# Tokenizer of a four-layer tower: loads ahead of the constants, two inputs prepared first, another order of joins, turns and projections

## The reference

```python
h = layernorm(x.reshape(b, t, j * 3), ln0_g, ln0_b).reshape(b, t, j, 3)
h = jax.nn.relu(conv2d(h, conv1_w, conv1_b, ((2, 2), (1, 1))))          # 128 -> 128 channels, 5 x 3 taps
h = layernorm(h.reshape(b, t, j * 3), ln0_g, ln0_b).reshape(b, t, j, 3)
h = jax.nn.relu(conv2d(h, conv2_w, conv2_b, ((2, 2), (0, 0))))          # 128 -> 128, 5 x 2
h = layernorm(h.reshape(b, t, j * 2), ln1_g, ln1_b).reshape(b, t, j, 2)
h = jax.nn.relu(conv2d(h, conv3_w, conv3_b, ((2, 2), (0, 0))))          # 128 -> 256, 5 x 2
h = h.reshape(b, 2 * t, j)
res = jnp.concatenate([h[:, :t, :], h[:, t:, :]], axis=2)
res = layernorm(res, ln1_g, ln1_b)
return res @ out_w + out_b
```

## Time and profile before

| | |
|---|---|
| runs of the kernel before | 3449.58, 3447.86, 3449.16 us, median 3449.16 |
| the profiled execution | 3440.6 us, span of the core 3438.8 us |
| granted TensorE clock over the span, mean | 0.969 |
| busy, share of the span | PE 91%, VectorE 62%, ScalarE 52%, GpSimd 34% |
| tokenizer phase | from 11.45 to 464.56 us |

### The profile page before, as it was taken

The page is one execution under the profiler, slowest core; times in us unless marked ns, Lnnn a source line. Parts: engine busy times, 40 slices in busy tenths (PEclk is TensorE's granted clock), DMA queues, the critical chain, the costliest instruction groups (busy, mean ns, idle before and its releaser), DMA issues. The chain is left out here.

```text
span 3438.8 us, 62285 instructions
## 1 busy us (share of the span) xinstructions
PE 3125.6 (91%) x23072; PEld 1955.5 (57%) x23093; DVE 2146.1 (62%) x4171; ACT 1800.0 (52%) x3978; POOL 1167.5 (34%) x1164
## 2 busy tenths in 40 slices
PE   5999979999999999998988979998699999998999
PEld 5999857446464646436755643334356666665444
DVE  5999735015353535327847744444699999974777
ACT  1323235565656564655644533334466666664666
POOL 3666511001010101104716612223477777760000
PEclk9999989999999999999999989998799999998999
DMA  2000000000000000000000022220100000003676
GB/s 86 15 20 10 1 18 12 1 8 1 6 1 6 1 6 1 6 7 2 2 9 1 1 58 56 56 57 16 24 10 5 4 4 5 4 1 43 72 68 65
DMA packets 75493, 66.48 MB, mean 19 GB/s; under 512 B 20406, under 2 KB 70681, under 8 KB 74777
## 3 DMA queue, kind: packets, MB, share of 16 engines
q1 hardware_dynamic: 75192, 62.49, 10.6%
HBM read 55.58 MB, written 2.51 MB: 17 GB/s over the span
## 5 line engine op out<-in xcount | busy, mean ns | idle before, releaser
L707 ACT ACTIVATE p_hidden<-p_hid_ps,net_bias 128x344 f32<-128x344 f32 x816 | 381.8, 548 | 226.4 <-PE p_hid_ps L654 167.9
L2427 POOL TENSOR_TENSOR p_qt<-p_qt,p_q_sum 97x512 f32<-97x512 f32 (+1 forms) x44 | 46.3, 1053 | 731.9 <-DVE p_q_sum L2381 731.9
L680 PE MATMUL p_y_ps<-p_hidden,net_down 128*64 128x344 f32 x1632 | 284.2, 466 | 1.6 <-DVE p_hidden L756 1.6
L654 PE MATMUL p_hid_ps<-xn,net_up 64*128 64x344 f32 x1248 | 241.4, 488 | 8.2 <-PEq L316 4.6
L2739 DVE TENSOR_TENSOR p_hid<-p_silu,p_pair_ps 128x344 f32<-128x344 f32 x288 | 134.7, 509 | 173.3 <-PE p_pair_ps L2688 95.3
L756 DVE TENSOR_TENSOR p_hidden<-p_hidden,p_row 128x344 f32<-128x344 f32 x384 | 175.4, 514 | 74.0 <-ACT p_hidden L707 50.7
L2720 ACT ACTIVATE p_silu<-p_pair_ps 128x344 f32<-128x344 f32 x288 | 116.0, 455 | 201.6 <-PE p_pair_ps L2677 201.6
L1899 POOL TENSOR_TENSOR p_rot<-p_rot,p_cross 128x512 f32<-128x512 f32 x128 | 160.4, 1274 | 126.8 <-DVE p_cross L2054 126.8
L680 PEld LDWEIGHTS p_y_ps<-p_hidden,net_down 128*64 128x64 f32 x1632 | 103.0, 136 | 156.8 <-issue 50.0
L1912 POOL TENSOR_TENSOR p_prob<-p_prob,p_total 128x1024 f32<-128x1024 f32 (+1 forms) x128 | 185.4, 1469 | 12.4 <-DVE p_total L2080 12.4
L654 PEld LDWEIGHTS p_hid_ps<-xn,net_up 64*128 64x128 f32 x1248 | 106.0, 189 | 128.6 <-ACT p_hidden L707 78.8
(11 more groups left out here) (451 smaller groups left out, 8091.4 us busy)
## 6 DMA issues: line engine op xcount, KB each, us to landing
p_row<-gated_rows SPq DMA_DIRECT2D x192, 86.0 KB, 2.9
p_row<-mark_rows SPq DMA_DIRECT2D x192, 86.0 KB, 10.2
p_x<-in_tok_x SPq DMA_DIRECT2D x16, 384.0 KB, 3.0
out<-h SPq DMA_DIRECT2D x12, 172.0 KB, 3.4
shared_value_pairs<-shared_values SPq DMA_DIRECT2D x16, 128.0 KB, 2.5
p_swapped<-xn SPq DMA_DIRECT2D x64, 32.0 KB, 1.9
p_kinds<-in_tok_c3w SPq DMA_DIRECT2D x1, 1280.0 KB, 9.3
thirds_fold<-in_L_fold SPq DMA_DIRECT2D x1, 1156.5 KB, 5.1
```

What stands on the lines that cost most here:

```text
L654: mm = pe.matmul(hid_ps[k % ring][:, 0:TILE], w_up[half(g), n, :], x[half(g), cols(t)], start=True, stop=not experts or by_rows)
L680: mm = pe.matmul(y_ps[u][half(g), 0:TILE], w_down[:, n, :], hid[k % hidden_ring][:], start=n == 0, stop=last and not experts)
L707: act.activation(hid[k % hidden_ring][:], hid_ps[k % ring][:, 0:TILE], func, bias=b_up[:, n:n + 1]).then_inc(act_done.sem, 1)
```

## The change

SP's first block now issues the first input, the bias columns, the first weights, the first norm's table and the second input into tiles that live before the phase (`TokenizerFront`). The other ten constants are issued in the tokenizer behind its remaining weights (`Constants`), and VectorE narrows five of them just ahead of its rounds. The block of casts goes. VectorE, ScalarE and GpSimd prepare inputs 0 and 1 ahead of the rounds; GpSimd waits for the remaining weights only in its first scale_last. Layer 2's shared sums have one buffer instead of two. In the rounds TensorE's order becomes first(s), project(s-4), second(s-1), third(s-2), turn(s-3); GpSimd's scale_last moves behind gather(1, s-1); VectorE joins layer 1 at the end of the round for t = s - 1 and centres the last norm behind join(0, s); ScalarE rectifies layer 1 at the end of the round and copies the turned tile at the head of the next.

```diff
+class TokenizerFront:
+
+
+    def __init__(self, stack, nc):
+        keep = lambda name, shape: stack.enter_context(nc.sbuf_tensor(f"tok_{name}", shape, F32))
+        self.x = [keep(f"x{r}", [P, 2 * HALVES, 192]) for r in range(2)]
+        self.kinds1, self.ln0 = keep("kinds1", [P, 5, TAPS_H, P]), keep("ln0", [P, 2, 192])
+        self.x_landed = [nc.alloc_semaphore(name=f"tok_x_landed{r}") for r in range(2)]
+        self.w_landed = nc.alloc_semaphore(name="tok_w_landed")
+
+
+class Constants:
+
+
+    def __init__(self, loaded, rest, narrowed):
+        self.loaded, self.rest, self.narrowed = loaded, rest, narrowed
+        self.total = 16 * (1 + len(rest))
...
-        common = [[ph.sb(f"common{k}{r}", [P, n]) for r in two] for k, n in enumerate((768, 640, 256))]
+        common = [[ph.sb(f"common{k}{r}", [P, n]) for r in two] for k, n in enumerate((768, 640))]
+        common.append([ph.sb("common2", [P, 256])] * 2)
...
-                for t in range(2):
-                    sp.dma_start(x_in[t][:], tower.dram["tok_x"][t]).then_inc(landed.sem, 16)
-                sp.dma_start(kinds1[:, 0:3], tower.dram["tok_c1w"]).then_inc(loaded_first.sem, 16)
-                sp.dma_start(ln0[:], tower.dram["tok_ln0"]).then_inc(loaded_first.sem, 16)
                 sp.dma_start(kinds2[:, 0:2], tower.dram["tok_c2w"]).then_inc(loaded_rest.sem, 16)
                 for buf, name in ((ln1_planes, "tok_ln1_planes"), (kinds3, "tok_c3w"), (ln1, "tok_ln1"),
                                   (ow, "tok_ow")):
                     sp.dma_start(buf[:], tower.dram[name]).then_inc(loaded_rest.sem, 16)
+                for buf, name in constants.rest:
+                    sp.dma_start(buf[:], tower.dram[name]).then_inc(constants.loaded, 16)
                 for t in range(2, steps):
                     if t >= 3:
                         sp.wait_ge(centered[0].sem, centered[0].at(t - 2))
-                    sp.wait_ge(landed.sem, landed.at(16 * t))
+                        sp.wait_ge(landed.sem, landed.at(16 * (t - 2)))
                     sp.dma_start(x_in[t % 3][:], tower.dram["tok_x"][t]).then_inc(landed.sem, 16)
             @block.tensor
...
-                for s in range(steps + 3):
+                for s in range(steps + 4):
                     if s < steps:
                         first(s)
                     if s == 1:
                         pe.wait_ge(loaded_rest.sem, loaded_rest.at(80))
                         pe.wait_ge(derived.sem, derived.at(2))
+                        pe.wait_ge(constants.loaded, constants.total)
+                    if 4 <= s:
+                        project(s - 4)
                     if 1 <= s < steps + 1:
                         second(s - 1)
-                    if s >= 3:
-                        turn(s - 3)
                     if 2 <= s < steps + 2:
                         third(s - 2)
-                    if s >= 3:
-                        project(s - 3)
+                    if 3 <= s < steps + 3:
+                        turn(s - 3)
...
                     table = lambda m: ln1[:, m:m + 1, :].to_broadcast([P, quad, 128])
+                    if t == 0:
+                        pool.wait_ge(loaded_rest.sem, loaded_rest.at(80))
...
-                pool.wait_ge(loaded_rest.sem, loaded_rest.at(80))
-                first_in(0)
-                for s in range(steps + 4):
+                for s in range(2):
+                    first_in(s)
+                for s in range(steps + 3):
                     if 2 <= s < steps + 2:
                         third_in(s - 2)
-                    if 3 <= s < steps + 3:
-                        scale_last(s - 3)
                     if s < steps:
                         gather(0, s)
-                    if s + 1 < steps:
+                    if 1 <= s < steps - 1:
                         first_in(s + 1)
                     if 1 <= s < steps + 1:
                         gather(1, s - 1)
+                    if 3 <= s:
+                        scale_last(s - 3)
                     if s < steps:
                         second_in(s)
...
-                inverse(0, 0)
+                for s in range(2):
+                    inverse(0, s)
                 for s in range(steps + 4):
+                    if 4 <= s:
+                        copy_turned(s - 4)
                     if 3 <= s < steps + 3:
                         share(2, s - 3)
-                    if 4 <= s:
-                        write(s - 4)
-                    if 2 <= s < steps + 2:
-                        rectify(1, s - 2)
-                    if 3 <= s < steps + 3:
                         rectify(2, s - 3)
                     if 2 <= s < steps + 2:
                         inverse(2, s - 2)
+                    if 1 <= s < steps - 1:
+                        inverse(0, s + 1)
                     if 3 <= s < steps + 3:
                         inverse(3, s - 3)
-                    if s + 1 < steps:
-                        inverse(0, s + 1)
                     if s < steps:
                         share(0, s)
+                    if 4 <= s:
+                        write(s - 4)
                     if 1 <= s < steps + 1:
                         share_lone(s - 1)
                     if s < steps:
...
                         inverse(1, s)
                     if 1 <= s < steps + 1:
                         share(1, s - 1)
-                    if 3 <= s < steps + 3:
-                        copy_turned(s - 3)
+                        rectify(1, s - 1)
...
-                dve.tensor_copy(h[:].rearrange("p (j t) -> p j t", t=SEQ)[:, :, 0],
-                                column("cls").to_broadcast([P, PAIRS]))
                 inputs(0)
-                dve.wait_ge(loaded_first.sem, loaded_first.at(32))
+                dve.wait_ge(front.w_landed, 32)
                 for side in two:
                     ins = dve.tensor_tensor(kinds1[:, 3 + side], kinds1[:, 2 * side], kinds1[:, 1], ALU.subtract)
                 ins.then_inc(kinds_made.sem, 1)
                 apply(0, 0, x_in[0])
                 dve.wait_ge(kinds_made.sem, kinds_made.at(1))
                 derive(0).then_inc(derived.sem, 1)
+                inputs(1)
+                dve.tensor_copy(h[:].rearrange("p (j t) -> p j t", t=SEQ)[:, :, 0],
+                                column("cls").to_broadcast([P, PAIRS]))
+                apply(0, 1, x_in[1])
                 dve.wait_ge(loaded_rest.sem, loaded_rest.at(80))
                 dve.tensor_tensor(kinds2[:, 2], kinds2[:, 0], kinds2[:, 1], ALU.add).then_inc(kinds_made.sem, 1)
                 derive(2)
                 dve.wait_ge(kinds_made.sem, kinds_made.at(2))
                 derive(1).then_inc(derived.sem, 1)
+                dve.wait_ge(constants.loaded, constants.total)
+                for narrow, of in constants.narrowed:
+                    dve.tensor_copy(narrow[:], of[:])
                 for s in range(steps + 3):
-                    if 2 <= s < steps + 2:
-                        join(1, s - 2)
-                    if 3 <= s:
-                        join(2, s - 3)
                     if 2 <= s < steps + 2:
                         dve.wait_ge(relu[1].sem, relu[1].at(s - 1))
                         measure(2, s - 2, act[1][s % 2])
                     if 3 <= s:
-                        dve.wait_ge(relu[2].sem, relu[2].at(s - 2))
-                        measure(3, s - 3, act[2][(s - 3) % 2])
-                    if s + 1 < steps:
+                        join(2, s - 3)
+                    if 1 <= s < steps - 1:
                         inputs(s + 1)
                     if 2 <= s < steps + 2:
                         apply(2, s - 2, act[1][s % 2])
                     if 3 <= s:
-                        center(3, s - 3, act[2][(s - 3) % 2])
-                    if s + 1 < steps:
+                        dve.wait_ge(relu[2].sem, relu[2].at(s - 2))
+                        measure(3, s - 3, act[2][(s - 3) % 2])
+                    if 1 <= s < steps - 1:
                         apply(0, s + 1, x_in[(s + 1) % 3])
                     if s < steps:
                         join(0, s)
+                    if 3 <= s:
+                        center(3, s - 3, act[2][(s - 3) % 2])
+                    if s < steps:
                         dve.wait_ge(relu[0].sem, relu[0].at(s + 1))
                         measure(1, s, act[0][s % 2])
                         apply(1, s, act[0][s % 2])
+                    if 1 <= s < steps + 1:
+                        join(1, s - 1)
...
-                consts = [(tower.ident, "ident"), (tower.center, "center"), (tower.average, "average"),
-                          (tower.rank8, "rank8"), (columns, "columns"),
-                          (tower.spread2, "spread2")]
-                consts += list(zip(wide, ("later", "place", "banish", "place2", "later2")))
-                if "h_in" in dram:
-                    consts.append((h, "h_in"))
-                for buf, name in consts:
```

(15 more changed lines are left out.)

27 lines of the change are left out of this document (18 added, 9 removed).

## The result

| | before | after |
|---|---|---|
| median of the runs (lowest to highest), same chip | 3448.51 us (3447.55 to 3449.58), 4 runs | 3472.66 us (3465.52 to 3474.05), 4 runs |
| ratio to before | | 1.0068, 95% interval 1.0056 to 1.008: 19 to 28 us slower |
| the profiled execution, span of the core | 3440.6, 3438.8 us | 3472.69, 3470.9 us |
| mean granted TensorE clock | 0.969 | 0.962 |
| first matmul of the tokenizer | 28.19 | 18.28 |

The time of the tokenizer splits into three parts. Up to the fourth first convolution the change gains 12.2 us. In the twelve rounds from there to the sixteenth it loses 35.6 (332.2 against 296.6). From the sixteenth to the end of the stage it gains 4.6 (72.4 against 77.0). Together the tokenizer ends 18.8 us later.

A forecast was written before the change was run, and what follows sets the result against it. VectorE's round, stretched by GpSimd collisions, was taken to set the 24.70 us step. Start -12.6, middle +25, clock +7 and end -3 gave +16, 3457 us; with 8.6 to the median, 3465, range 3431 to 3480.

The forecast's parts named there:

- wait at the turn, twelve rounds: Middle steps: TensorE waits 2.5 us at each turn, step 26.8 against 24.70, +2.1 in each of 12 rounds, +25 us.
- clock behind the waits: Middle steps: TensorE at half clock after some turn waits, 0.6 us per wait, +7 us, ends 0 and +20.
- the end: From the last first convolution to the tokenizer's end: -3 us, ends 0 and -6.
- The chain to the turn: Loop from first(s) over VectorE, ScalarE and GpSimd to turn(s-3): ready at 15.65 us, TensorE there at 13.1.
- The start: Tokenizer's opening: TensorE starts 9.8 us earlier, its stop before the second input shrinks 2.1, clock 0.7; 12.6 us gained.
- my one in three: Middle steps: the guess that one turn wait in three costs TensorE clock, 0.6 us per step.
- Both rivals on the clock, none and each: Turn waits cost no clock (+10, 3459 us) or each costs it (+30, 3479 us); no separate chance for either.
- the upper end, 27.5 a step: Middle steps with left-out collisions, such as layer 0's gather meeting the next input's scaling: 27.5 us a step, +34.
- The turn ready in time: Rival, middle steps: scalings collide less or not, step 24.3, TensorE packed, -21, 3428 us; chance 0.28, nearly in time included.
- The halfway case: Rival, middle steps: step near 25.4, -7, 3442 us; within the 0.18 shared with no clock cost and a slightly shorter step.
- The start giving nothing: Rival, tokenizer's opening: weights land late, first weights at 18 as before, +27, 3476 us; chance 0.02.
- The rule on collisions: VectorE and GpSimd share SBUF interfaces; VectorE's two-input or two-port instructions collide with GpSimd: step 26.8, without collision 24.3.

The follow-up runs named there:

- the version that packs TensorE: The changed kernel with GpSimd's scale_last(s-3) put ahead of gather(1, s-1): 3429.47 us, ratio 0.9935; repeated on another chip, 3424.83 us.
- the first version: The kernel before with only the change's loads, casts and preparation of both inputs, old order of the rounds: 3438.87 us, ratio 0.9959.
- the wide sum: An unused GpSimd sum of 128x512 per step, added to the version with scale_last ahead of gather(1, s-1): 3426.56 us, one run.
- that kernel: The changed kernel with GpSimd's first_in(s+1) moved behind gather(1, s-1) and scale_last(s-3): 3517.74 us, ratio 1.0181.

## Why the prediction was right

Forecast 3465 us and slower, with a chance of 0.54; measured 3472.66 and slower by 0.56 to 0.8%. The terms of the sum against the traces (us):

| term | forecast | measured |
|---|---|---|
| first matmul | -9.8 | -9.9 |
| stop ahead of the second first convolution | -2.1 | -2.0 |
| clock of the start, and the rest to the fourth | -0.7 | -0.3 |
| wait at the turn, twelve rounds | +25 | +28.3: eleven of 2.14 and a first of 4.8 |
| clock behind the waits | +7 | +7.2 |
| the end | -3 | -4.6 |
| tokenizer | +16 | +18.8 |

**The chain to the turn** was the step on which the forecast stood, and it held link by link. Counted from the first convolution's end at 258.71: join over at 4.3 (forecast 4.2), centring at 6.9 (6.8), second gather at 11.7 (11.7), scalings at 15.6 (15.6), the turn at 15.65 (15.65). TensorE stood ready for the turn at 13.3 (13.1). The step without a loss of clock was 26.83 for 26.8. The collisions came as costed, the first two centring instructions each with one GpSimd instruction, the product behind the gather, the scalings in turn with product and sum. Removing the second gather from ahead of the scalings took off the whole wait, in the version that packs TensorE; moving the centring out of the first collision took off 2.0 of the 2.4, 0.7 of it by a second collision that went with it.

**The start** was right in its mechanism, and it is shown to be independent: alone it gives -12.4 at the tokenizer's end. That its terms agree to 0.1 us is in part luck: with the same start the first matmul stands between 18.28 and 19.71 in the profiles here, and the fourth first convolution begins at 78.76 in the changed kernel but at 77.02 with the start alone.

**The clock** cost 7.2 us beyond the steps of 26.83: four of the eleven regular waits and the first, long one were followed by a fall, close to my one in three. That share was a guess from three rows, and its closeness is luck as much as reading: in the version with only the rounds, three of the eleven were followed by one, and the clock cost 6.4 us. Both rivals on the clock, none and each, are refuted by either profile. A stretch behind one of them, in the busy table of the changed kernel:

```profile
245.80:252.00 6.20, 6.14 (x22) 4.64 (x22) 5.18 (x25) 2.91 (x9) 3.24 (x4) 0.72 0.01 1
```

6.20 x 0.28 is 1.7 us, the price taken from rows 5. The mean in the middle was below 1.00, as forecast.

**What was too small.** First, the term "12 rounds of 2.1": it took a settled rhythm for all twelve, and the first of them starts from a packed step, with a late share and the gather in a collision (one of that kind I had named and left for the upper end, 27.5 a step). It held once, for 2.7 us over a regular round. Second, the turn from the profiled execution to the median. I added 8.6 us, the distance of the kernel before; but the changed kernel's rest behind the tokenizer is 2987.5 us, 13.3 above that of before, so 4.7 more than that distance. With 2.8 from the tokenizer's sum this is 7.5 of the 7.7 by which 3465 was low. An execution whose unchanged remainder is unusually short had been my base, and one profile did not show it. (That the rest of before was a short draw is likely and not shown, as said above.)

**The rivals.** The turn ready in time (3428) did not happen, but its number is what the version with the scaling first gives: 24.2 a step for my 24.3, and 3424.8 and 3429.5 us. It needs one exchange on one queue. The halfway case, a step near 25.4 and 3442, is nearly the version with the later centring (24.82, 3440.32). The start giving nothing is refuted, by the first version.

**The rule on collisions.** The prediction cited the Trainium skill ("GPSIMD Engine Reference", Specifications) for VectorE's two-input and two-port instructions colliding with GpSimd. The rows agree, and the single instructions show how: a scaling took 1.32 us beside a sum of 1.29, and 0.88 beside a memset of 0.52. The Trainium skill's page "SBUF — State Buffer" (SBUF: two separate sides) says that whichever of the two starts first has the shared ports for its whole instruction and the other waits for its end. The scaling of 1.32 agrees with that: it starts 0.08 us behind the sum and ends 0.11 behind it. The scaling of 0.88 stood behind two instructions: its row starts while a sum runs that ends at 260.15, the memset begins at 260.10 and goes ahead of it. So the start of a row does not tell which of the two is served first. Joins, which read PSUM, and statistics took the same beside GpSimd as alone (0.68 to 0.69 and 1.10 to 1.14 us) in all these traces.

What stays open: by which of the waits the clock falls. It fell behind four of eleven equal stops of 2.4 us, and I tried nothing that tells them apart. Open too is what holds the step at 24.69 in the version with the turn moved.

## What to carry to other kernels

Before a step is moved behind another on one queue, write out the loop from the first engine's output round to its next start, with each neighbour's longest instruction in it, and compare the sum with the slot; here a chain of 15.65 us against a slot of 13.3 cost more than the 12.4 us that a better start had gained. In these runs short VectorE scalings from SBUF to SBUF went in lock-step with whatever GpSimd ran, one for one, so place such scalings beside GpSimd's idle time or keep them off the way to the engine that is the bound, and put GpSimd's work for that engine ahead of work that others can wait for. When a change has two independent parts, time each: here one was worth -12 us, the other +30, and with one exchange both became gains (3429.47 us for both together, 3438.87 for the start alone).

## What the runs showed of the hardware that was not expected

- A stop of TensorE costs about 0.2 us more than the idle time that its row shows: with a wait of 2.39 at full clock the step is 26.83 against 24.23, 2.60 more; with 0.37 it is 24.82, 0.59 more. Most of it is the overlap of 0.17 us between rows without a stop (258.32 + 0.39 against 258.54), which a stop loses.
- What a collision costs VectorE goes by how many of its instructions meet one of GpSimd's, and by the length of those, not by its own work: four scalings of 128x128, 1.1 us together when alone, took 2.7 beside two sums of 1.13 and 1.29; and of the four of 128x192 beside the wide sum and the gather, three were held, at 1.32, 0.78 and 0.88, where one with GpSimd idle takes 0.37.
- Stops of 0.87 and 2.48 us within 3.2 us, in each step, brought the mean granted clock to 0.89 in steps of a profiled execution (one step, from 153.59, stayed at 1.00), where single stops of 2.4 left 0.96 to 1.00 in a step; and that kernel's five runs scatter from 3505 to 3555 us.
